# Feed-forward of a gated cross-attention block: all experts for every token, or only the two chosen ones

## The reference, cut to what matters

```python
# x: 4096 rows of 256, normalised; E = 8 experts, I = 128 hidden
scores = sigmoid(x @ router_weight.T)            # (4096, 8)
choice = scores + correction_bias
# the better of two groups of 4 experts (sum of its two best), then the top 2 in it
comb = one_hot(top2) * scores / sum_of_the_two   # zero for six of eight experts
g = einsum('th,ehi->tei', x, w_gate); u = einsum('th,ehi->tei', x, w_up)
y = einsum('tei,eih->teh', silu(g) * u, w_down)
routed = einsum('teh,te->th', y, comb)
shared = (silu(x @ sw_gate) * (x @ sw_up)) @ sw_down
out = x_in + tanh(g_ffn) * (routed + shared)
```

## Time and profile before

| what | value |
|---|---|
| median of 3 runs | 1168.97 us (1168.93 to 1169.73) |
| profiled execution: span from first to last instruction | 1167.4 us |
| TensorE busy, share of the span | 1137.5 us, 97% |
| VectorE busy | 859.4 us, 74% |
| ScalarE busy | 647.0 us, 55% |
| GpSimd busy | 383.2 us, 33% |
| mean granted TensorE clock | 0.995 |
| DMA | 34.92 MB, mean 30 GB/s |

### The profile page before, as it was taken

One profiled execution on the slowest core, in us unless ns is written; L12 is line 12 of the kernel. 1 busy time (PEld: TensorE's weight loads), 2 busy tenths in 40 slices (PEclk: granted clock), 3 DMA queues, 4 the chain that ended last, 5 costly groups with the idle time before them and its releaser, 6 DMA issues. The chain is left out here.

```text
span 1167.4 us, 26523 instructions
## 1 busy us (share of the span) xinstructions
PE 1137.5 (97%) x8481; PEld 1095.4 (94%) x8481; DVE 859.4 (74%) x2059; ACT 647.0 (55%) x1561; POOL 383.2 (33%) x577
## 2 busy tenths in 40 slices
PE   5899999999999999999999999998999999999998
PEld 4899999999999999999999999997999999999998
DVE  5777777777777777777777777776876767767766
ACT  4766566666656666566666666655433333333333
POOL 2512112122121221212212121211366666666663
PEclk9999999999999999999999999999899999999999
DMA  9300000000000000000000000000112121121121
GB/s 298 112 15 5 0 3 3 0 3 0 3 1 1 3 0 3 0 3 3 0 3 0 3 3 0 0 1 1 37 47 83 47 75 60 50 85 45 54 84 64
DMA packets 23861, 34.92 MB, mean 30 GB/s; under 512 B 3744, under 2 KB 20240, under 8 KB 21776
## 3 DMA queue, kind: packets, MB, share of 16 engines
q1 hardware_dynamic: 23536, 34.33, 8.7%
q10 hardware_dynamic: 288, 0.13, 0.0%
HBM read 30.13 MB, written 4.33 MB: 30 GB/s over the span
## 5 line engine op out<-in xcount | busy, mean ns | idle before, releaser
L245 POOL TENSOR_TENSOR prob<-prob,rinv 128x333 f32<-128x333 f32 x128 | 94.6, 739 | 617.7 <-DVE rinv L474 617.7
L450 DVE TENSOR_REDUCE nmax<-ps_s 128x1 f32<-128x333 f32 x256 | 127.6, 499 | 65.6 <-PE ps_s L548 65.5
L320 ACT ACTIVATE prob<-ps_s,nmax 128x333 f32<-128x333 f32 x256 | 137.3, 536 | 63.8 <-DVE nmax L450 62.3
L904 ACT ACTIVATE th<-ps_gu 128x256 f32<-128x256 f32 x144 | 55.3, 384 | 211.8 <-PE ps_gu L1165 211.8
L1165 PE MATMUL ps_gu<-xt_hi,gu_hi 128*128 128x256 f32 x576 | 164.7, 286 | 1.8 <-DVE xt_lo L962 1.6
L1165 PE MATMUL ps_gu<-xt_lo,gu_hi 128*128 128x256 f32 x576 | 164.0, 285 | 0.0
L1165 PE MATMUL ps_gu<-xt_hi,gu_lo 128*128 128x256 f32 x576 | 164.0, 285 | 0.0
L430 DVE SCALAR_TENSOR_TENSOR k_lo<-ps_k,vecs,k_hi 128x334 fp32r<-128x334 f32 x128 | 72.5, 566 | 82.7 <-ACT k_hi L302 82.7
L330 ACT ACTIVATE o_hi<-ps_qa,vecs 128x256 fp32r<-128x256 f32 x127 | 60.4, 475 | 131.1 <-PE ps_qa L548 131.1
L857 POOL TENSOR_TENSOR f_lo<-act_h,f_hi 128x256 fp32r<-128x256 f32 x131 | 97.0, 741 | 107.3 <-ACT f_hi L898 107.3
L1085 DVE SCALAR_TENSOR_TENSOR act_a<-th,ps_gu 128x256 f32<-128x256 f32 x144 | 60.0, 417 | 87.1 <-ACT th L904 87.0
(11 more groups left out here) (162 smaller groups left out, 3652.2 us busy)
## 6 DMA issues: line engine op xcount, KB each, us to landing
wide_w<-comb_rows SPq DMA_DIRECT2D x16, 1024.0 KB, 4.6
out_dram<-y_out SPq DMA_DIRECT2D x16, 256.0 KB, 2.1
x_all<-in_x_dram SPq DMA_DIRECT2D x1, 3584.0 KB, 17.4
raw<-in_L_xattn_Wkv_dram SPq DMA_DIRECT2D x4, 512.0 KB, 7.1
ctx_in<-in_ctx_dram SPq DMA_DIRECT2D x16, 77.0 KB
raw<-in_L_xattn_Wq_dram SPq DMA_DIRECT2D x2, 512.0 KB, 7.0
raw<-in_L_xattn_Wo_dram SPq DMA_DIRECT2D x2, 512.0 KB, 10.3
raw<-in_L_ffn_w_gate_dram SPq DMA_DIRECT2D x4, 256.0 KB, 4.4
```

The lines of the kernel that those rows point to most:

```text
L245: pool.tensor_tensor(prob[:, h % 2, 0, 0:KEYS], prob[:, h % 2, 0, 0:KEYS], rinv[:, h % 2, 0:1].to_broadcast([P, KEYS]), ALU.mult).then_inc ...
L320: act.activation(prob[:, h % 2, i, 0:KEYS], ps_s[i][:, 0:KEYS], ACT.Exp, bias=nmax[:, h % 2, i:i + 1], accum_out=rsum[:, h % 2, i:i + 1]). ...
L450: dve.tensor_reduce(nmax[:, h % 2, i:i + 1], ps_s[i][:, 0:KEYS], AX.X, ALU.max, negate=True).then_inc(max_ready, 1)
```

## The change

The function ffn is replaced by sparse_ffn. Attention changes a little: DVE also computes mean and variance of each batch's new x (in steps 3 to 5 of the next batch) and keeps them in mv_all; the special case that normalised the first feed-forward pair inside attention goes. The feed-forward's raw weights are loaded in 10 DMAs instead of 14 with another layout.

The first sweep (16 duos of two token tiles) computes the shared expert and the router, with tokens as rows now: tokens are the stationary operand and the weights (256 or 272 columns) the moving one. ACT normalises (two activations per duo) instead of DVE. Routing is done for a chunk of eight tiles at a time, and ranks the first and second choice separately. Each token gets a destination row for each of its two choices: experts have regions in DRAM, and the row in the region is a running count, from products with a triangular matrix of ones (count). POOL then writes the rows out with indirect DMAs: for the first choice weights, token id, normalised token and the residual with the shared expert's part (516 floats), for the second choice without the residual (260 floats). All sends of the second choices of a chunk go first. The ring of rows in SBUF has 24 tiles; a tile's slot is free again when its chunk's sends have landed.

After that a table is made of which expert each of 40 tiles serves in each choice, and where its rows start. The second sweep goes over the 40 tiles of the first choice: SP loads 128 rows, PE turns them, one expert's gate/up and down products follow, DVE adds the weighted result to the residual, and POOL writes the sums to the second choice's place (acc) with an indirect DMA. The third sweep does the same for the second choice, adds acc, and POOL writes the rows to the output by token id. The two sweeps are one pipeline over 40 duos. The expert's number is read from the table into a register of PE, and picks the weights.

The core of the diff:

```diff
-def ffn(nc, t, x_all, ident, z, raw_gu, raw_down, raw_in):
+def sparse_ffn(nc, t, x_all, ident, mv_all, raw_gu, raw_sh, raw_dn, raw_in):
...
+        DUOS = TILES // TT
+        CHUNK = 8
+        SLOTS = 3 * CHUNK
+        XTILES = TILES + EXP
+        XDUOS = RANKS * XTILES // TT
+        NB = 2 * CHUNK
+        NY = CHUNK
...
+            sp.wait_ge(empty_out, 16 * 3 * EXP)
+            for c in range(CHUNKS):
+                sp.wait_ge(sent[c], 16 * RANKS * CHUNK)
+            sp.wait_ge(tab_ready, 1)
+            for tile in range(XTILES):
+                fetch(tile)
+            held = [(tile, fetch(tile)) for tile in range(XTILES, XTILES + NB)]
+            for s in range(NY):
+                sp.wait_ge(y_sent[s], 16 * len(range(s, XTILES, NY)))
+            for tile, start in held:
+                fetch_sum(tile, start)
...
+            def send(c):
+                pool.wait_ge(route, ROUTE * (c + 1))
...
+                for k in (1, 0):
+                    width, region = ((ROW0, d0), (ROW1, d1))[k]
+                    for tile in range(c * CHUNK, (c + 1) * CHUNK):
+                        if k == 0:
+                            pool.wait_ge(resid_ready, tile // TT + 1)
+                        pool.indirect_dma_start(region[:, :], bass.IndirectOffsetOnAxis(ap=dest[:, tile, k:k + 1], axis=0),
+                                                rows[:, slot(tile), 0:width], None, bounds_check=EXP * REGION - 1,
+                                                oob_is_err=False).then_inc(sent[c], 16)
...
+            for c in range(CHUNKS):
+                if c >= SLOTS // CHUNK:
+                    place_ids(c)
+                while n < min(len(PIECES), CDUOS * (c + 1)):
+                    split_lo(n)
+                    n += 1
+                send(c)
...
+            def send_row(tile):
+                rank_no = tile // XTILES
+                y = tile % NY
+                region, limit = ((acc, EXP * REGION - 1), (out, ROWS - 1))[rank_no]
+                pool.wait_ge(e_to, tile + 1)
+                pool.wait_ge(e_y, tile + 1)
+                pool.indirect_dma_start(region[:, :], bass.IndirectOffsetOnAxis(ap=to_row[:, y:y + 1], axis=0), yout[:, y, :],
+                                        None, bounds_check=limit, oob_is_err=False).then_inc(y_sent[y], 16)
...
+            def normalise(tile):
+                act.wait_ge(shift_ready, tile // CHUNK + 1)
+                if tile >= SLOTS:
+                    act.wait_ge(sent[(tile - SLOTS) // CHUNK], 16 * RANKS * CHUNK)
...
+            def shared_gate_up(d):
+                pe.wait_ge(xtlo_ready, d + 1)
+                if d == 0:
+                    pe.wait_ge(shlo_ready, 2)
+                else:
+                    pe.wait_ge(h_done, d)
+                    pe.wait_ge(parts_ready, d)
...
+            def expert(tile):
+                rank_no, j = divmod(tile, XTILES)
+                at = P + rank_no * HALF + j
+                return pe.value_load(tab_row[0:1, at:at + 1], min_val=0, max_val=EXP - 1)
+
+            def e_gate_up(n, which):
...
+                for i in range(TT):
+                    e = which[i]
+                    k = 0
                     for c in range(FC):
...
+                        at = c * TOK + i * P
+                        for x, w in ((xt_hi, gu_hi), (xt_hi, gu_lo), (xt_lo, gu_hi)):
+                            mm = pe.matmul(ps_g[:, n % 2, i * TOK:(i + 1) * TOK], x[:, n % 2, at:at + P],
+                                           w[:, c, bass.ds(e, 1), :].rearrange("p o n -> p (o n)"), start=k == 0, stop=k == 3 * FC - 1)
+                            k += 1
```

More of the change, by code:

```diff
@@ L66, in sem @@
             return ctx.enter_context(nc.semaphore(name))
-        def tiles(b):
-            return TT if isinstance(b, int) and b == BATCH else TT + 1
         QO, KVO, OO = 0, FC * INNER, 3 * FC * INNER
@@ L404, in aggregate @@
             def aggregate(b):
-                for i in range(tiles(b)):
+                for i in range(TT + 1):
                     rows = P if i < 2 else MEDIA
@@ new lines, in sparse_ffn @@
+        below = sb("below", [P, EXP])
+        mine = sb("mine", [P, EXP])
+        natural = sb("natural", [P, EXP])
+        first = sb("first", [P, EXP])
+        facts = sb("facts", [P, 3, EXP])
+        mine_facts = sb("mine_facts", [P, 3, EXP])
+        region0 = sb("region0", [P, EXP])
+        table = sb("table", [P, 3])
+        diag = sb("diag", [P, P], F32R)
+        tab_row = sb("tab_row", [1, 2 * P], mybir.dt.int32)
+        skip = sb("skip", [P, P])
+        xin = rows[:, 0:NB, :]
@@ L794, in ffn, with weights, slot, uses @@
+        def weights(piece, part):
+            kind, a, b = piece
+            if kind == "gu":
+                w = {"raw": raw_gu, "hi": gu_hi, "lo": gu_lo}[part]
+                return w[:, a, b:b + 2, :]
+            w = {"raw": raw_dn, "hi": dn_hi, "lo": dn_lo}[part]
+            return w[:, a:b, :]
+        def slot(tile):
+            return tile % SLOTS
+        def uses(tile, ring):
+            return tile // ring + 1
         block = ctx.enter_context(nc.Block())
@@ L814, in _ @@
[L814 to L827 removed]
+            sp.dma_start(bias_half[:, :], t["L0_ffn_correction_bias"].unsqueeze(0).to_broadcast([P, EXP])).then_inc(vec_in, 16)
@@ L885, in _ @@
+            pool.wait_ge(skip_ready, 1)
+            for tile in range(4):
+                address(tile)
+            for tile in range(RANKS * XTILES):
+                send_row(tile)
+                if tile + 4 < RANKS * XTILES:
+                    address(tile + 4)
         @block.scalar
         def _(act):
-            def tokens_hi(p, par):
-                act.wait_ge(x_turned, p + 1)
-                _wait(act, gu_done, NU * (p - 1))
-                act.activation(xt_hi[:, par, :, :].rearrange("p c n -> p (c n)"), ps_x[:, :], ACT.Copy).then_inc(xthi_ready, 1)
@@ new lines, in split_hi @@
+            def split_hi(n):
+                act.activation(weights(PIECES[n], "hi"), weights(PIECES[n], "raw"), ACT.Copy).then_inc(whi_ready, 1)
+            act.wait_ge(raw_in, 16 * RAW_DMAS)
+            act.activation(sh_hi[:, :, 0:SH], raw_sh[:, :, :], ACT.Copy).then_inc(sh_ready, 1)
+            for tile in range(2 * TT):
+                normalise(tile)
+            tokens_hi(0)
+            act.wait_ge(vec_in, 32)
+            act.activation(gf[:, :], gf[:, :], ACT.Tanh).then_inc(gate_ready, 1)
@@ new lines, in _ @@
+            for d in range(DUOS + 2):
+                if d + 2 < DUOS:
+                    normalise(TT * (d + 2))
+                    normalise(TT * (d + 2) + 1)
+                if d + 1 < DUOS:
+                    tokens_hi(d + 1)
+                if d >= 1 and d % CDUOS == 0 and d <= DUOS:
+                    logit_gate(d // CDUOS - 1)
+                if 0 <= d - 1 < DUOS:
+                    hidden_hi(d - 1)
+                if d < DUOS:
+                    gate(d)
+                for n in W_AT.get(d, ()):
+                    split_hi(n)
@@ new lines, in e_hidden_hi @@
+            def e_hidden_hi(n):
+                act.wait_ge(e_h_turned, n + 1)
+                if n >= 2:
+                    act.wait_ge(e_down, n - 1)
+                act.activation(ht_hi[:, n % 2, :], ps_h[:, 0:TOK], ACT.Copy).then_inc(e_hthi, 1)
+            act.wait_ge(down_done, DUOS)
+            e_tokens_hi(0)
+            for n in range(XDUOS + 1):
+                if n + 1 < XDUOS:
+                    e_tokens_hi(n + 1)
+                if n < XDUOS:
+                    e_gate(n)
+                if n >= 1:
+                    e_hidden_hi(n - 1)
@@ new lines, in _, with steps @@
+            for c in range(1, CHUNKS):
+                shifts(c)
+            dve.wait_ge(gate_ready, 1)
+            dve.tensor_scalar(tgf_half[:, :], gf[:, :], 0.5, None, ALU.mult).then_inc(gate_ready, 1)
+            pending = []
+            for d in range(DUOS + 2):
+                def steps(count):
+                    for _ in range(min(count, len(pending))):
+                        pending.pop(0)()
+                if d + 1 < DUOS:
+                    tokens_lo(d + 1)
+                steps(2)
+                if d < DUOS:
+                    hidden(d)
+                steps(2)
+                if 0 <= d - 1 < DUOS:
+                    hidden_lo(d - 1)
+                steps(2)
+                if d >= 2:
+                    residual(d - 2)
+                if d < DUOS and d % CDUOS == CDUOS - 1:
+                    pending += routing(d // CDUOS)
+                if d >= DUOS - 1:
+                    steps(9)
@@ new lines, in _ @@
+            turn_tokens(0)
+            for d in range(DUOS + 2):
+                if d + 1 < DUOS:
+                    turn_tokens(d + 1)
+                if d < DUOS:
+                    shared_gate_up(d)
+                if 0 <= d - 1 < DUOS:
+                    turn_hidden(d - 1)
+                if d >= 2:
+                    shared_down(d - 2)
```

(3 more changed lines are left out.)

1053 lines of the change are left out of this document (606 added, 447 removed).

## The result

The changed kernel takes 1140.74 us (median of 4 runs, 1139.18 to 1141.93) against 1169.35 before: a ratio of 0.9756, 95% interval 0.9742 to 0.9769, so 2.4% faster. The forecast was 1120 us.

A forecast was written before the change was run, and what follows sets the result against it. TensorE's instruction stream bounds the kernel. Second stage's first product at 952, plus 152 for 40 duos, plus 14 for cold start, stall and drain: 1118, with 1.6 around it 1120 us; own range 1085 to 1150, overall 1062 to 1192.

The forecast's parts named there:

- First sweep's period: First sweep, 16 duos: VectorE bounds at 4.6 us, with contention 5.1 us per duo, range 4.5 to 6.
- T = 1.25 us for one indirect DMA: POOL's issue time per 128-row send, the middle between SP's issue at 0.39 and a store's landing at 2.1 us.
- (a): Rival: cheap issue, near 0.4 us per indirect DMA, and register loads covered; end at 1065 us; chance 0.2.
- (b): Rival: POOL's issue queue slower, before and in the second stage; 1206 us at 2.1 per indirect DMA; chance 0.22.
- Landing: Sent rows land after 2.1 us; first scatters landing over 3 us after issue would show the prediction wrong.
- POOL never catches up: First sweep's sends: a chunk costs POOL 20 + 4 us, one is supplied in 20; last send out at 945.
- ACT's wait for landing: First sweep: ACT's normalise of tile 24 waits for chunk 0's rows to land, holding ACT and TensorE 7 us.
- the sign for the register loads: Second stage: TensorE's idle time ends by its own sequencer; if POOL or a DMA ends it, loads aren't the cause.
- Second and third sweep: 3.8 per duo: 40 duos, TensorE leading: 2.8 us of work plus two register loads at 0.5 each; 152 us.
- rival (c): Second stage: register loads at 1.1 make 5.0 us per duo, or slow DMA 4.6; ending 1140 to 1175; chance 0.1.
- Drain and last scatter: 6: End of the kernel: 6 us added for the drain and the last scatter.
- rival (d): TensorE's clock stays at half because of its gaps: 5.2 us per duo, 1176 us; chance 0.03.

The follow-up runs named there:

- one_more_sem: Changed kernel with one unused semaphore declared, so later semaphores are numbered one higher, same work; 1127.33 us, ratio 0.9647.
- extra_sends: Changed kernel plus 32 further indirect sends of 128, 64 or 32 rows into a DRAM region nobody reads; 1175.06 us, ratio 1.0061.
- fixed_experts: Changed kernel with TensorE's expert numbers fixed when the program is built, so no register loads on TensorE; 1131.44 us, ratio 0.9672.
- extra_load: Changed kernel with SP loading one more unused table value per tile of the third sweep; 1141.98 us, ratio 0.9766.
- sp_tail: Changed kernel with the last eight tiles' results stored by SP in an unread region, POOL's last indirect DMA eight tiles earlier; 1121.72 us, ratio 0.959.
- sittings 1, 2 and 5: Groups of kernels timed together on one chip (not on record, 14, 5); the first holds the changed kernel; late completions in all their kernels.
- sittings 3 and 4: Groups of kernels timed together on one chip (15 and 14), without the changed kernel; late completions in none.
- late_two: Changed kernel sending tile by tile, first eight tiles' rows released duo by duo, last two chunks' second choices after the fetches; 1110.45 us, ratio 0.9495.
- late_seconds: Changed kernel with the last chunk's first choices sent first and its second choices no longer awaited by the fetches; 1118.17 us, ratio 0.9561.
- paced: Changed kernel with a small POOL addition, waited for, after each of the 64 sends; 1181.85 us, ratio 1.0104.

## Why the prediction was right, and where it was off

The time fell in the forecast's own range, 20.7 us above its value. The forecast's sum against the changed kernel's profile: first product of the second stage 975.4 instead of 952 (+23.4); from there to the last result 146.6 instead of 160 (-13.4); from there to the end 15.4 instead of 6 (+9.4); between span and median 3.3 instead of 1.6 (+1.7). Together 21, and 1140.7 - 1120 is 20.7. Direction, the main mechanism and its largest price held; two sizes were off and cancelled in part, which is luck, and one thing was missing. Without late completions the same work took 1127.3 (one_more_sem), 7 above the forecast.

- **Attention.** 708.0 of 711 us against 709.4: the ten small VectorE steps cost nothing, as said.
- **TensorE's work.** Forecast 179 us less, measured 154. From 816 on TensorE is busy for 189 us instead of 157: 65 in the 16 duos of the first sweep, 4.1 each instead of 2.8, at clocks of 0.5 to 0.88, and 3.1 each in the 40 duos behind it. Its share of the span is 86%, not near 80%.
- **First sweep's start.** First product 822.7, forecast 821; first send 858.8, forecast 857. Right.
- **First sweep's period.** Forecast 5.1, range 4.5 to 6. Undisturbed duos come in a pattern of 3.8, 3.8, 5.3 and 4.7 us (hidden products of one_more_sem): 4.4 on the mean. The long ones are those with routing, and VectorE is the bound, as forecast: busy 92% at 844 to 862 of one_more_sem. I had added its short steps as if each waited for the one before, at 0.25 us each; at 894.5 in one_more_sem three of them start 0.11 us apart. Contention with POOL's splits is real and rare: logits, 0.21 us long in one_more_sem, takes 3.45 beside the splits of 909.55 to 913.28 and ends with them (lines below). The Trainium skill, page "SBUF — State Buffer", section "Who interferes with whom", has descriptor generation on GpSimd starved by VectorE, but not beside tensor_tensor and tensor_reduce, which are most of VectorE's work here. A send's mean is 0.985 us at 889 to 911 of one_more_sem, with VectorE busy 84% of the time, and 0.975 us when it is idle (943 to 965 of the changed kernel). One part in a hundred: these traces don't show the starving.

```profile
892.34 0.21 DVE L1155 TENSOR_TENSOR logits<-lparts 128x64 f32<-128x64 f32 x1
...
909.92 3.45 DVE L1155 TENSOR_TENSOR logits<-lparts 128x64 f32<-128x64 f32 x1
```

- **T = 1.25 us for one indirect DMA.** 1.28, and by the instruction, not the row. The middle between SP's 0.39 and the landing at 2.1 was a lucky choice, but extra_sends confirms what hung on it. Rivals (a) and (b) both needed another T and fall.
- **Landing.** I had 2.1 us and took more than 3 for the first scatters as a sign of being wrong. Measured in one_more_sem, where the landings can be told: 2.5 to 3.1 us for the first sends, median 3.3 for the scatters of the second sweep. The sign is half there; its price is in the 11.3 instead of 7 us below and in the change of rank.
- **POOL never catches up.** Nearly: it waited 4.7 us for chunk 1's routing and 8.9 for chunk 2's. 4.7 of this stays without the hold-up.
- **ACT's wait for landing.** It was there, at the tile that was named, 13.9 instead of 7 us: the sweep was faster than forecast, so it came to the wait earlier.
- **The missing step: TensorE's completions held back while POOL sends.** The prediction had TensorE, ACT and POOL coupled by semaphores that arrive at once. From 893.7 to the next hidden products 19.2 us passed, where one_more_sem takes 5.3. (Beside chunk 0's sends they were late too, but the wait for landing covers it: both kernels take 17.6 us there.) Chunk 2's routing and sends then come late: the last send ends at 964.1 against 955.4 in one_more_sem. These 8.7 and another 3.4 in the second stage (146.6 against 143.2 from its first product to the last result) are nearly the whole 12.5 between the two spans. Of the 23.4 us by which the second stage was late, 8.7 are thus the hold-up; the rest are 1.8 of the first send, 4.7 of waiting for chunk 1, 1.9 from the larger T on 64 sends, 2 of splits and what stands around them, and 4.3 for landing, fetch, copies and first product (11.3 instead of 7).
- **TensorE idle 43 us before the second stage.** From 940.6 to 971.8 it has no instruction; 31 us. The sends ended later, and the sweep too. In 974 to 1056 its idle time ends with nothing that the profile shows ("issue", 7.4 us in 20 waits), as the sign for the register loads said.
- **Second and third sweep: 3.8 per duo.** 3.4 in the second (3.3 in one_more_sem) and about 3.6 in the third before its last, quick duos. A register load is 0.25 us, not 0.5: fixed_experts gives 0.23 per duo in all, since POOL follows at 3.2. In the third sweep the bound is one that I had not named: SP, with a load and two issues in 1.68 us per tile, 3.4 per duo; extra_load shows it. The time lies at the low end of rival (c)'s 1140 to 1175, but not by its cause: a duo takes 3.4 to 3.6 us, not 5.0 or 4.6. The change of rank cost 5.7 us more than a period (9.0), forecast 5.
- **Drain and last scatter: 6.** Measured 15.4. POOL had 6 us of scatters in arrears when the last result was there (1122.0 to 1127.96), and its drain then took 9.2 us more. sp_tail separates the two.
- **Clock.** 1.00 in 980 to 1050 in spite of gaps; rival (d) falls. In the hold-up and in POOL's stretch alone it is at 0.5 to 0.7, as the earlier trace rows let expect.

Not settled: why the completions are late. Shown is that lateness of several us comes only in rows of sends (in the changed kernel at 866.1 to 882.1 and, from 893.5, 4 us behind the first of chunk 1's sends, until 912.2, 3 us behind the last; at 887 to 889, between two rows, none is late; among the scatters of the second and third sweep it is 2.4 us at most), that it hits TensorE's semaphores and SP's plain register instructions alike, that VectorE and ACT run their own instructions at their usual durations in between, and that all six kernels of sittings 1, 2 and 5 have it and none of the seven of sittings 3 and 4. Chip 14 is on both sides, so it is not the chip alone. Whether it is the sitting or the program's layout would be shown by the changed kernel, timed beside one_more_sem; that run is missing. Transfers are no sufficient cause, as one_more_sem moves the same 134 GB/s in that window. All executions here were recorded, the timed ones too, since each has its span and its clock. The Trainium skill, page "NOTIFIC — the notification-queue block", section "Overflow: three behaviours, one of which stalls the engine", says that the block which takes the engines' records can be set to hold back its producers when a queue of records fills, until software empties it. A fixed 0.70 us for instructions that do next to nothing would fit a record that has to wait, and software that empties slowly would fit a state of the sitting; no run here tells this apart from a cause that would be there without recording.

## What to carry to other kernels

An indirect DMA costs POOL 0.9 to 1 us plus 0.3 for 32 rows as for 128, so count instructions, and ask of each whether it must stand ahead of the barrier: here eight that need not were worth 9.2 us, and sixteen, with the early release, 16.9 (late_two against one_more_sem). When a kernel's time moves by 1% and its edit can't explain it, time the unchanged kernel again beside it, in the same sitting; a steady kernel before (1168.8 to 1169.5 in all sittings) does not show that the changed one is steady. Here the same work took 1140.7 and 1127.3, and late_seconds, sp_tail and extra_load would have been misread without a reference that has no late completions. And a stage in which TensorE (3.3 us per duo), POOL (3.2) and, in the third sweep, SP (3.4) are that close has three bounds: taking one away, the register loads, gave 0.23 of its 0.5 us.

## What the runs showed that was not expected

- TensorE's completions up to 15.6 us late during rows of sends, in 6 of the 13 kernels with this sweep, and 13.4 us between two kernels that do the same work. The timed runs of those six spread over 2.6 to 10.1 us, those of the others over 1.5 to 3.1.
- POOL's drain at the end of a block: 0.85 us after attention, where POOL had issued no DMA, and 8.57 to 9.2 us behind its last work once it had issued indirect DMAs, also when the last of them had landed 7 us before (sp_tail). In the kernel before it ends 0.1 us behind POOL's last work.
- An instruction of POOL followed by an indirect DMA that waits for it: 0.8 us between them for an addition on one column (paced). Where the scatter waits only for a sum made four tiles earlier, as in the second stage, it starts 0.17 us behind the instruction before it.
